# Gated cross-attention with an aux table: the value table as bf16 halves, and moves in the opening, the reloads and the last tiles

## Chip, cores and metric

The kernel runs on 1 core of a Trainium2 chip. Its time is the device time of one execution, in microseconds (us). All engine names are those of the profile: PE is TensorE, DVE is VectorE, ACT is ScalarE, POOL is GpSimd, SP issues most transfers.

## What is computed

The reference, cut to what matters:

```python
# x: (8, 224, 2048), ctx: (8, 750, 512), mask: (224, 750)
q  = layernorm(x)                                     # 32 heads of 64, ctx gives 8 key/value heads
p  = softmax(q_head @ ctx_head.T / 8 + mask)
x  = x + tanh(g_xattn) * (p @ ctx_head)               # keys and values are the same rows
h  = layernorm(x)
query = h @ Wq.T
router = (query @ Wr.T) @ (aux_keys @ Wr.T).T / sqrt(48) + log_rel     # 512 slots, the 8 highest are kept
w  = softmax(query @ aux_keys.T / 8 + log_rel over those 8)
aux = (w @ aux_values) @ Wvd.T @ Wvu.T                # 2048 -> 128 -> 2048
gate = f(var(h), gelu(h @ Wu1.T + bu1) @ Wu2.T + bu2)
x  = x + tanh(g_ffn) * (h + gate * aux)
```

## The kernel before

Each engine has its own program, written out by hand; they meet at semaphores only. What an engine does is in the order of its function, and a wait holds everything behind it.

**Attention.** The 224 rows of a batch are 128 "top" rows and 96 "rest" rows. A window is one batch and one key head (64 of them); a window has seven units of 128 query rows: four of top rows and three of rest rows. The loop variable `k` runs over the units, `place(k)` gives window and unit `m`. For a unit PE makes the scores (`score_main` L896, `score_mid` L907), DVE adds the mask and takes the maximum (L1289), ACT the exponential (L709), PE turns the result (L919, L926), ACT copies it from PSUM (L705), POOL makes the low half, that is the fp32 value less its upper 16 bits (L578), and PE multiplies both halves with the values (L943, L944, L949). Rows are normalized for a pair of windows: `norm_top` on ACT (L672), `norm_rest` on ACT (L678); for batch 0 ACT does the first 128 columns of the rest rows and POOL the other 384 (L571). The statistics of batch 0's rest rows are averaged over partitions by two small products on PE (L993, L995), with DVE steps L1206 to L1213 between and behind them. The finished rest rows go to a scratch tensor in DRAM, `spill` (L423, 12 transfers per batch).

**Aux part.** 14 tiles of 128 rows: eight of top rows, kept in SBUF, and six read back from `spill` (L485, L488). The value table `v2 = aux_values @ Wvd.T` is summed once, in `sum_v2` (L1021): eight pieces of two 128-row blocks, each piece in one of three staging slots (`load_piece`, L466 and L467), fp32 with fp32. These slots and the lower half of the tile area lie over buffers of attention. Per tile PE does `sum_wide` (L972), `sum_query` (L986), `turn_h` (L959), `route` (L1076, L1080, L1081), `turn_w` (L1060), `sum_z` (L1066); all wide operands are split into a high and a low half. DVE does the top-8 selection (`select`), ACT `gelu` (L772) and `weigh` (the softmax weights, L776), each with its own function table.

**Results.** A tile's result is `base` (ACT, L751, 128x2048) plus four parts of 512 columns: `aux_part` on PE (L1050), added by `finish` on DVE (L1391). The table `FINISH` says in which loop step `t` which tiles are finished; the parts stand at fixed places `i` = 0 to 7 of the step. All parts share PSUM bank 7, so that part `n+1` waits until DVE has added part `n`; the last two tiles, behind the loop, have banks of their own (`TAIL_BANKS`). SP stores a finished tile; quarters of the last two tiles go out from SP and ACT.

The pieces of code on which the steps below rest, where a sentence does not say it:

```python
            sum_v2(range(0, 2))      # PE, behind pe.wait_ge(x_added, GROUPS)
            sum_wide(0, 2)
            sum_query(0, 2)
            turn_h(1, 1)
            sum_v2(range(2, 4))
```

## Time and profile before

| | |
|---|---|
| median of 3 runs | 1185.97 us (1185.53 to 1186.67) |
| profiled execution, its own time | 1187.15 us |
| its span, first to last instruction | 1185.3 us |
| busy: PE, PEld | 1158.6 us (98%), 914.1 us (77%) |
| busy: DVE, ACT, POOL | 944.8 us (80%), 918.7 us (78%), 888.7 us (75%) |
| chain of waits | PE 73%, POOL 19%, DVE 3%, DMA 2% |
| DMA | 95.09 MB, mean 80 GB/s |
| from issue to landing, median | piece of the value table 5.7 us, spilled tile read back 7.4 us, spill row 2.2 us |

PEld is the loading of weights, which overlaps PE. The chain of waits follows the last instruction back to what released it, step by step; a share of it is time in which nothing else could have started the next step. Attention ends at about 888 us, the loop over tiles runs from 919 to 1171 us.

### The profile page before, as it was taken

The numbers are of one execution on the slowest core, as the hardware profiler recorded it, in microseconds if no ns is written. First come the engines' busy times: TensorE is split into PE (matmuls) and PEld (weight loads), VectorE is DVE, ScalarE is ACT, GpSimd is POOL, SyncE is SP. The second block draws the span as 40 slices with busy tenths as digits, with TensorE's granted clock in tenths as the row PEclk, the third lists the DMA queues.
The fourth block names the chain that finished last, engine by engine and source line by source line (L and its number), as shares of the span: only waits on it lengthen the run. The fifth ranks groups of instructions, "written<-read, shape, count | busy, mean of one in ns | idle before, by whom it ended". The sixth has DMA issues, their size and how long they took to land.

```text
span 1185.3 us, 35321 instructions
## 1 busy us (share of the span) xinstructions
PE 1158.6 (98%) x14642; PEld 914.1 (77%) x14642; DVE 944.8 (80%) x2255; ACT 918.7 (78%) x1230; POOL 888.7 (75%) x800
## 2 busy tenths in 40 slices
PE   5999999999999999999999999999999999999997
PEld 3888888888888888888888888888887666555553
DVE  5988888888888888888888888888864899666765
ACT  5898988888998989989899889988871444655544
POOL 5899999999999999999999999999981111403222
PEclk9999999999999999999999999999999999999999
DMA  9421231233114212321321231131227200011223
GB/s 346 124 79 48 57 116 41 55 78 100 41 42 117 73 43 61 110 55 48 98 73 43 57 71 41 42 70 53 77 95 244 108 2 1 1 72 72 107 107 142
DMA packets 60736, 95.09 MB, mean 80 GB/s; under 512 B 35234, under 2 KB 44450, under 8 KB 56483
## 3 DMA queue, kind: packets, MB, share of 16 engines
q1 hardware_dynamic: 59858, 91.79, 25.5%
q8 instruction: 118, 1.93, 0.7%
q10 hardware_dynamic: 720, 1.05, 0.3%
q14 instruction: 40, 0.32, 0.1%
HBM read 71.75 MB, written 20.97 MB: 78 GB/s over the span
## 4 chain that ended last, share of the span: by engine, by line
PE 73%; POOL 19%; DVE 3%; DMA 2%; issue 1%; ACT 1%; SPq 1%; DVEq 0%; POOLq 0%
POOL arena L578 14%; PE psum L896 12%; PE psum L919 12%; PE psum L972 11%; PE psum L926 6%; PE psum L907 6%; PE psum L949 5%; PE psum L943 5%; PE psum L944 5%; PE psum L1050 3%; POOL arena L546 2%; PE psum L986 2%; PE psum L959 2%; PE psum L874 2%; POOL arena L595 1%
## 5 line engine op out<-in xcount | busy, mean ns | idle before, releaser
L578 POOL TENSOR_TENSOR arena<-arena 128x768 bf16<-128x768 f32 x448 | 652.7, 1472 | 45.2 <-ACT arena L705 43.3
L1289 DVE CUSTOM_DVE_ANT_0 arena<-psum,arena 128x750 f32<-128x750 f32 x448 | 420.5, 939 | 129.7 <-PE psum L907 124.1
L705 ACT ACTIVATE arena<-psum 128x768 f32<-128x768 f32 x448 | 362.5, 809 | 89.4 <-PE psum L926 89.4
L709 ACT ACTIVATE arena<-arena,neg_max 128x750 f32<-128x750 f32 x448 | 410.8, 917 | 4.2 <-DVE neg_max L1289 4.2
L896 PE MATMUL psum<-arena 128*128 128x512 bf16 x896 | 272.8, 385 | 0.0
L919 PE MATMUL psum<-ident,arena 128*128 128x128 f32 x1792 | 269.2, 273 | 0.0
L943 PEld LDWEIGHTS psum<-arena 128*128 128x128 bf16 (+1 forms) x2688 | 194.7, 98 | 57.5
L944 PE MATMUL psum<-arena 128*128 128x64 bf16 (+1 forms) x2688 | 222.0, 193 | 0.0
L943 PE MATMUL psum<-arena 128*128 128x65 bf16 (+1 forms) x2688 | 221.7, 194 | 0.0
L944 PEld LDWEIGHTS psum<-arena 128*128 128x128 bf16 (+1 forms) x2688 | 178.5, 98 | 53.2
L919 PEld LDWEIGHTS psum<-ident,arena 128*128 128x128 f32 x1792 | 207.0, 141 | 5.5 <-ACT arena L709 1.1
L926 PE MATMUL psum<-ident,arena 128*128 128x128 f32 x896 | 171.5, 273 | 0.1
L907 PE MATMUL psum<-arena 128*128 128x238 bf16 x896 | 167.8, 268 | 1.8 <-DVE neg_max L1289 0.9
L972 PE MATMUL psum<-arena 128*128 128x512 bf16 x672 | 161.4, 384 | 0.0
L949 PE MATMUL psum<-arena 128*128 128x65 bf16 (+1 forms) x2688 | 160.0, 194 | 0.9 <-POOL arena L578 0.9
L972 PEld LDWEIGHTS psum<-arena 128*128 128x128 bf16 x672 | 63.6, 96 | 75.0 <-issue 0.8
L949 PEld LDWEIGHTS psum<-arena 128*128 128x128 bf16 (+1 forms) x2688 | 114.9, 98 | 1.5 <-POOL arena L578 1.4
L926 PEld LDWEIGHTS psum<-ident,arena 128*128 128x128 f32 x896 | 112.1, 141 | 0.6 <-ACT arena L705 0.4
L685 ACT ACTIVATE arena<-psum 128x512 bf16<-128x512 f32 x56 | 33.3, 597 | 99.1 <-PE psum L959 99.0
L1232 DVE SCALAR_TENSOR_TENSOR arena<-psum,r_den,arena 128x64 f32<-128x64 f32 x448 | 97.4, 277 | 2.3
L546 POOL TENSOR_TENSOR arena<-arena 128x750 bf16<-128x750 f32 x64 | 92.3, 1442 | 0.0
L896 PEld LDWEIGHTS psum<-arena 128*128 128x128 bf16 x896 | 88.1, 98 | 5.3
(160 smaller groups left out, 1270.9 us busy)
## 6 DMA issues: line engine op xcount, KB each, us to landing
arena<-in_k_t SPq DMA_DIRECT2D x128, 187.5 KB, 3.2
arena<-in_v_rows SPq DMA_DIRECT2D x64, 192.0 KB, 2.5
out<-arena SPq DMA_DIRECT2D x12, 1024.0 KB, 3.9
arena<-in_x_top SPq DMA_DIRECT2D x8, 1024.0 KB, 5.3
arena<-in_x_rest SPq DMA_DIRECT2D x8, 768.0 KB, 4.6
spill<-arena SPq DMA_DIRECT2D x96, 64.0 KB, 2.2
arena<-spill SPq DMA_DIRECT2D x6, 1024.0 KB, 7.4
arena<-in_w_t SPq DMA_DIRECT2D x4, 1024.0 KB, 19.4
```

The source lines that it names most:

```text
L578: pool.tensor_tensor(p_lo[:, n % RING, :], p_sb[:, n % RING, :], high(p_sb[:, n % RING, :]), ALU.subtract).then_inc(p_split, 1)
L705: act.activation(p_sb[:, n % RING, :], flat_ps[:, turned_at(n):turned_at(n) + CW], ACT.Copy).then_inc(evac_a, 1)
L709: act.activation(s_sb[:, n % RING, 0:CTX], s_sb[:, n % RING, 0:CTX], ACT.Exp, bias=neg_max[:, n % 4, :], scale=-1.0).then_inc(exped, 1)
L896: pe.matmul(flat_ps[:, score_at(n) + cols.start:score_at(n) + cols.stop], q_t[:, pair % 2, half, turn, :], kk, start=(i == 0), stop=(i == 1))
L907: mm = pe.matmul(flat_ps[:, score_at(n) + cols.start:score_at(n) + cols.stop], q_t[:, g // 2 % 2, half, turn, :], kk, start=(i == 0), stop ...
L919: pe.transpose(flat_ps[:, at:at + 128], s_sb[:, n % RING, c * 128:(c + 1) * 128], ident[:, :])
L926: mm = pe.transpose(flat_ps[:, at:at + 128], s_sb[:, n % RING, c * 128:(c + 1) * 128], ident[:, :])
L943: pe.matmul(o, hi, v_hi[0:rows, u, c, :], start=(c == 0), stop=False, skip_group_check=True)
L944: pe.matmul(o[:, 0:D], hi, v_lo[0:rows, u, c, :], start=False, stop=False, skip_group_check=True)
L949: mm = pe.matmul(o, lo, v_hi[0:rows, u, c, :], start=False, stop=(c == NCH - 1), skip_group_check=True)
L972: mm = pe.matmul(psum[:, 2, :], h[:, j, kk, :], w, start=(k == 0 and n == 0), stop=(k == KC - 1 and n == 2))
L1289: dve.tensor_tensor_reduce(s_sb[:, n % RING, 0:CTX], flat_ps[:, score_at(n):score_at(n) + CTX], mask_sb[:, max(n % UNITS - REP + 1, 0), :] ...
```

## The change

1. The value table is summed from halves. GpSimd makes the low halves of each piece (`split_piece`: three subtractions), after the last batch's rows have been spilled; PE runs three bf16 products where one fp32 product was. PE no longer waits for the load of a piece but for `v2_split`. The pieces stand at other places: 2, 3, 2, 1 instead of 2, 2, 2, 2.
2. SP reads the first three spilled tiles back after the last piece's load, not between the pieces.
3. Opening: ACT's `norm_rest` of batch 0 and its `norm_top(1)` go to POOL, under the new semaphores `rest_first` and `top_second`; the second averaging product comes after the first unit's scores.
4. In step t=1 ACT does `weigh(0)` ahead of `gelu(0)`.
5. Result part 5 is added before the split and the next rows of the step, not after them.
6. Tile 11 is finished behind the loop, with tiles 12 and 13; twelve parts there use seven banks in turn; DVE's and ACT's last steps are in another order.

```diff
-FINISH = {8: (0, 1), 9: (2, 3), 10: (4, 5), 11: (6, 7), 12: (8, 9), 13: (10, 11), 14: (12, 13)}
+FINISH = {8: (0, 1), 9: (2, 3), 10: (4, 5), 11: (6, 7), 12: (8, 9), 13: (10,), 14: (11, 12, 13)}
...
+        TAIL = FINISH[TILES]
+        TAIL_SEQ = (7, 0, 1, 3, 4, 5, 2, 7, 0, 1, 3, 4)
+        TAIL_BANKS = {(u, n): TAIL_SEQ[4 * i + n] for i, u in enumerate(TAIL) for n in range(4)}
...
@@ SP
             for i in range(STAGE_SLOTS, KC // 2):
                 sp.wait_ge(v2_piece, i - STAGE_SLOTS + 1)
                 load_piece(i)
-                if i - STAGE_SLOTS in (0, 2, 4):
-                    u = (i - STAGE_SLOTS) // 2
-                    sp.dma_start(x2b[:, u, :], spill[128 * u:128 * u + 128]).then_inc(x2_loaded[u], 16)
-            sp.wait_ge(v2_piece, KC // 2)
-            for i in range(3, B_TILES):
+            for i in range(B_TILES):
+                if i == 3:
+                    sp.wait_ge(v2_piece, KC // 2)
                 sp.dma_start(x2b[:, i, :], spill[128 * i:128 * i + 128]).then_inc(x2_loaded[i], 16)
...
@@ POOL
-            for j in range(NB):
-                pool.tensor_scalar(xn_rest[:, j, 2 * D:], xb[:, 0, j, 2 * D:], ln_scale[:, 1 + j:2 + j], ln_bias[:, 1 + j:2 + j],
-                                   ALU.mult, ALU.add).then_inc(rest_widened, 1)
+            for cols, done in ((slice(0, 2 * D), rest_first), (slice(2 * D, KV * D), rest_widened)):
+                for j in range(NB):
+                    pool.tensor_scalar(xn_rest[:, j, cols], xb[:, 0, j, cols], ln_scale[:, 1 + j:2 + j], ln_bias[:, 1 + j:2 + j],
+                                       ALU.mult, ALU.add).then_inc(done, 1)
...
+                if m == 2 and window == -1:
+                    pool.tensor_scalar(xn_top[:, 1, :], xa[:, 0, 2 * GW:4 * GW], ln_scale[:, 0:1], ln_bias[:, 0:1],
+                                       ALU.mult, ALU.add).then_inc(top_second, 1)
...
+            def split_piece(i):
+
+                slot = i % STAGE_SLOTS
+                pool.wait_ge(v2_loaded[slot], 32 * (1 + i // STAGE_SLOTS))
+                if i >= STAGE_SLOTS:
+                    pool.wait_ge(v2_piece, i - STAGE_SLOTS + 1)
+                for kk in range(2):
+                    pool.tensor_tensor(av_lo[:, slot, kk, :], av_stage[:, slot, kk, :], high(av_stage[:, slot, kk, :]),
+                                       ALU.subtract).then_inc(v2_split, 1)
+                pool.tensor_tensor(wvd_lo[:, slot], wvd_stage[:, slot], high(wvd_stage[:, slot]), ALU.subtract).then_inc(v2_split, 1)
+
+            pool.wait_ge(spilled[(BATCH - 1) % 3], 16 * REP * NB * ((BATCH - 1) // 3 + 1))
+            for i in range(KC // 2):
+                split_piece(i)
...
@@ ACT
-                if k == -4:
-                    for j in range(NB):
-                        norm_rest(0, j)
...
-                if m == 6 and window == -1:
-                    norm_top(1)
...
-                gelu(t - 1)
                 if t == 1:
                     weigh(0)
+                gelu(t - 1)
...
-            store_quarter(TILES - 2, 1)
             act.wait_ge(last_clipped, 1)
             act.activation(last_col[:, 4:5], last_col[:, 3:4], ACT.Exp, bias=scal_neg[:, 2:3], scale=scal_neg[:, 1:2]).then_inc(last_exped, 1)
+            store_quarter(TILES - 2, 1)
...
@@ PE
-            pe.wait_ge(own_step, 3)
-            pe.matmul(psum[:, 3, 0:NB], quad[:, :], own_sum[:, :], start=True, stop=True).then_inc(own_spread, 1)
...
+                if k + 5 == 0:
+                    pe.wait_ge(own_step, 3)
+                    pe.matmul(psum[:, 3, 0:NB], quad[:, :], own_sum[:, :], start=True, stop=True).then_inc(own_spread, 1)
...
-                    pe.wait_ge(v2_loaded[i % STAGE_SLOTS], 32 * (1 + i // STAGE_SLOTS))
+                    slot = i % STAGE_SLOTS
+                    pe.wait_ge(v2_split, 3 * i + 3)
                     for kk in range(2):
+                        wide = high(wvd_stage[:, slot, kk, :])
                         for m in range(4):
-                            mm = pe.matmul(psum[:, 6, m * 128:(m + 1) * 128], av_stage[:, i % STAGE_SLOTS, kk, m * 128:(m + 1) * 128],
-                                           wvd_stage[:, i % STAGE_SLOTS, kk, :], start=(i == 0 and kk == 0 and m == 0),
+                            cols = slice(m * 128, (m + 1) * 128)
+                            values = high(av_stage[:, slot, kk, cols])
+                            pe.matmul(psum[:, 6, cols], values, wide, start=(i == 0 and kk == 0 and m == 0), stop=False, skip_group_check=True)
+                            pe.matmul(psum[:, 6, cols], values, wvd_lo[:, slot, kk, :], start=False, stop=False, skip_group_check=True)
+                            mm = pe.matmul(psum[:, 6, cols], av_lo[:, slot, kk, cols], wide, start=False,
                                            stop=(i == KC // 2 - 1 and kk == 1), skip_group_check=True)
                     mm.then_inc(v2_piece, 1)
...
-            sum_v2(range(2, 4))
+            sum_v2(range(2, 5))
             sum_wide(0, 3)
             sum_query(0, 3)
             turn_h(1, 2)
-            sum_v2(range(4, 6))
+            sum_v2(range(5, 7))
             turn_h(1, 3)
             route(0)
-            sum_v2(range(6, 8))
+            sum_v2(range(7, 8))
...
-            for i in range(4):
-                if i == 0:
+            for i in range(4 * len(TAIL)):
+                if i == 1:
                     turn_w(TILES - 1)
                 aux_part(TILES, i)
-                if i == 1:
+                if i == 3:
                     sum_z(TILES - 1)
...
@@ DVE
                 split_z(t - 1)
+                finish(t, 5)
                 late_stats(t, 6)
                 if t + 1 < TILES:
                     split_h(t + 1, 2)
                 if t + 2 < TILES:
                     stage_h(t + 2, 0)
-                finish(t, 5)
...
             finish(TILES, 0)
+            finish(TILES, 1)
             dot(TILES - 1)
-            finish(TILES, 1)
-            split_z(TILES - 1)
+            finish(TILES, 2)
+            finish(TILES, 3)
             dve.wait_ge(last_exped, 1)
...
-            finish(TILES, 2)
+            split_z(TILES - 1)
+            finish(TILES, 4)
             dve.wait_ge(last_exped, 2)
...
-            for i in range(3, 8):
+            for i in range(5, 4 * len(TAIL)):
                 finish(TILES, i)
```

PE's order where attention has ended, before: `wr_rows` is the router's product, L1021 are the value table's products, L972 the wide products of tile 0.

```order
L959 MATMUL psum<-ident,arena 128x128 x3
L1092 MATMUL psum<-arena,wr_rows 64x512 [waits rk_ready]
L1021 MATMUL psum<-arena 128x128 [waits v2_loaded0,x_added]
L1021 MATMUL psum<-arena 128x128 x7
L1021 MATMUL psum<-arena 128x128 [waits v2_loaded1]
L1021 MATMUL psum<-arena 128x128 x7
L972 MATMUL psum<-arena 128x512 [waits w1_split,h_split]
```

And of the change; the three lines L1060 to L1062 (high by high, high by low, low by high) come eight times per piece, two pieces in a row, before the same wide products.

```order
L993 MATMUL psum<-ident,arena 128x128 x3
L1134 MATMUL psum<-arena,wr_rows 64x512 [waits rk_ready]
L1060 MATMUL psum<-arena 128x128 [waits v2_split,x_added]
L1061 MATMUL psum<-arena 128x128
L1062 MATMUL psum<-arena 128x128
```

The products stand where they stood, with three instructions for one, and their wait is now for GpSimd. On POOL, behind the low half of the keys, the change has these (before, the statistics of tile 3, `ga<-mv_all`, follow at once):

```order
L629 TENSOR_TENSOR keys_lo<-arena,keys_hi 128x512 [waits keys_split]
L638 TENSOR_TENSOR arena<-arena 128x512 [waits v2_loaded0,spilled1]
L638 TENSOR_TENSOR arena<-arena 128x512
L640 TENSOR_TENSOR arena<-arena 128x256
L638 TENSOR_TENSOR arena<-arena 128x512 [waits v2_loaded1]
L638 TENSOR_TENSOR arena<-arena 128x512
L640 TENSOR_TENSOR arena<-arena 128x256
```

The first of them waits for the last spilled rows (`spilled1`). The third place is DVE in a step with results, before:

```order
L1395 TENSOR_TENSOR arena<-psum,arena 128x128 [waits z_ready]
L1279 TENSOR_TENSOR arena<-psum,arena 128x512 [waits h_hi_done]
L1260 TENSOR_SCALAR arena<-arena,mv_all,rstd_all 128x512 [waits h_turned,rstd2_done]
L1391 SCALAR_TENSOR_TENSOR arena<-psum,aux_scale,arena 128x512 [waits aux_summed] x2
L1370 TENSOR_TENSOR arena<-psum,arena 128x512 [waits dotted,w1_quarter]
```

and of the change, where one of the two additions stands ahead of the split (L1319) and the next rows (L1300):

```order
L1435 TENSOR_TENSOR arena<-psum,arena 128x128 [waits z_ready]
L1431 SCALAR_TENSOR_TENSOR arena<-psum,aux_scale,arena 128x512 [waits aux_summed]
L1319 TENSOR_TENSOR arena<-psum,arena 128x512 [waits h_hi_done]
L1300 TENSOR_SCALAR arena<-arena,mv_all,rstd_all 128x512 [waits h_turned,rstd2_done]
L1431 SCALAR_TENSOR_TENSOR arena<-psum,aux_scale,arena 128x512 [waits aux_summed]
L1410 TENSOR_TENSOR arena<-psum,arena 128x512 [waits dotted,w1_quarter]
```

## Rows read from the trace of the kernel before

**Rows 1.** Chain of waits, opening; columns: start us, us, what.

```profile
14.43 0.59 PE psum L995 x2
15.01 0.88 PE psum L896 x2
15.89 0.41 PE psum L907 x2
...
16.47 0.94 DVE arena L1289
...
23.50 0.73 PE psum L919 x4
...
29.21 0.44 PE psum L919 x4
```

**Rows 2.** Windows, opening; columns: stretch, us, busy per engine, PEclk, DMA share, GB/s.

```profile
22.00:24.00 2.00, 2.00 (x10) 1.62 (x9) 1.13 (x3) 1.92 (x4) 1.25 (x1) 1.00 1.03 430
```

**Rows 3.** Timeline, opening; start us, us, engine line op [idle before <-releaser].

```profile
17.11 1.97 POOL L571 TENSOR_SCALAR arena<-arena,ln_scale,ln_bias 128x384 f32<-128x384 f32 x3
18.28 1.25 ACT L678 ACTIVATE arena<-arena,ln_bias,ln_scale 128x128 f32<-128x128 f32 x3
22.75 1.47 POOL L578 TENSOR_TENSOR arena<-arena 128x768 bf16<-128x768 f32 x1 [2.82 <-ACT arena L705]
27.56 0.20 PEld L926 LDWEIGHTS psum<-ident,arena 128*128 128x128 f32 x2 [0.36 <-ACT arena L705]
```

**Rows 4.** Timeline, change of stage.

```profile
893.82 3.84 PE L1021 MATMUL psum<-arena 128*128 128x128 f32 x32
899.50 0.33 SPq L466 DMA_DIRECT2D arena<-in_av_t  x1
903.21 2.05 PE L1021 MATMUL psum<-arena 128*128 128x128 f32 x16 [0.21 <-DMA arena<-in_wvd_t]
915.47 3.84 PE L1021 MATMUL psum<-arena 128*128 128x128 f32 x32 [0.40 <-DMA arena<-in_wvd_t]
921.91 0.69 DVE L1343 CUSTOM_DVE_ANT_0 arena<-arena 128x512 f32<-128x512 f32 x1 [2.14 <-ACT arena L772]
924.06 0.66 PE L1060 MATMUL psum<-ident,arena 128*128 128x128 f32 x4 [0.31 <-ACT arena L776]
```

**Rows 5.** Windows, step t=10: us, PE, PEld, DVE, ACT, POOL busy, PEclk.

```profile
1083.43:1106.29 22.86, 22.33 (x140) 12.52 (x137) 15.55 (x29) 11.83 (x16) 6.15 (x18) 1.00 0.23 93
```

**Rows 6.** Timeline, change of stage, VectorE beside GpSimd.

```profile
889.39 1.60 POOL L606 TENSOR_SCALAR arena<-arena 128x512 f32<-128x512 f32 x1 [4.71 <-PE psum L1087]
891.04 1.47 DVE L1260 TENSOR_SCALAR arena<-arena,mv_all,rstd_all 128x512 f32<-128x512 f32 x1
```

**Rows 7.** Chain of waits, change of stage and t=10.

```profile
905.66 9.76 DMA arena<-in_wvd_t
...
1094.53 0.86 PE psum L1076 x2
...
1105.62 0.67 PE psum L1050 x3
1106.29 1.34 PE psum L986 x24
```

**Rows 8.** Groups of GpSimd, whole span: line, names, shapes, count, busy us, mean ns, idle.

```profile
L578 POOL TENSOR_TENSOR arena<-arena 128x768 bf16<-128x768 f32 x448 | 652.7, 1472 | 45.2 <-ACT arena L705 43.3
...
L595 POOL TENSOR_TENSOR arena<-arena 128x512 bf16<-128x512 f32 x16 | 16.8, 1050 | 0.2
```

**Rows 9.** Timeline, step t=10.

```profile
1101.76 0.54 DVE L1260 TENSOR_SCALAR arena<-arena,mv_all,rstd_all 128x512 f32<-128x512 f32 x1
...
1103.01 0.84 PE L1050 MATMUL psum<-arena 128*128 128x512 bf16 x3 [0.53 <-DVE arena L1391]
```

**Rows 10.** Timeline, tail.

```profile
1172.04 0.63 ACT L772 ACTIVATE arena<-arena 128x512 f32<-128x512 f32 x1 [1.72 <-DVE arena L1370]
...
1178.11 3.38 DVE L1391 SCALAR_TENSOR_TENSOR arena<-psum,aux_scale,arena 128x512 f32<-128x512 f32 x5
```

More of the change, by code:

```diff
@@ L187, in flamingo_block @@
         wvd_stage = slots[:, :, 2 * NSLOT:2 * NSLOT + 2 * VB].rearrange("p s (k n) -> p s k n", k=2)
+        lo_at = stage_at + STAGE_SLOTS * (2 * NSLOT + 2 * VB)
+        lo_slots = arena[:, lo_at:lo_at + STAGE_SLOTS * (NSLOT + VB)].bitcast(BF16).rearrange("p (s n) -> p s n", s=STAGE_SLOTS)
+        av_lo = lo_slots[:, :, 0:2 * NSLOT].rearrange("p s (k n) -> p s k n", k=2)
+        wvd_lo = lo_slots[:, :, 2 * NSLOT:2 * NSLOT + 2 * VB].rearrange("p s (k n) -> p s k n", k=2)
+        assert lo_at + STAGE_SLOTS * (NSLOT + VB) <= used["ffn"]
         v2 = carve("ffn", [128, 4, VB])
@@ L250, in flamingo_block @@
         rest_normed = sem("rest_normed")
+        rest_first = sem("rest_first")
+        top_second = sem("top_second")
         spilled = [sem(f"spilled{i}") for i in range(3)]
@@ L285, in flamingo_block @@
         v2_ready = sem("v2_ready")
+        v2_split = sem("v2_split")
         preact_done = sem("preact_done")
@@ L382, in parts_before, with tail_user @@
             return 4 * ORDER.index(u) + n
-        TAIL_BANKS = {(TILES - 2, 0): 7, (TILES - 2, 1): 0, (TILES - 2, 2): 1, (TILES - 2, 3): 3,
-                      (TILES - 1, 0): 4, (TILES - 1, 1): 5, (TILES - 1, 2): 2, (TILES - 1, 3): 7}
+        TAIL = FINISH[TILES]
+        TAIL_SEQ = (7, 0, 1, 3, 4, 5, 2, 7, 0, 1, 3, 4)
+        TAIL_BANKS = {(u, n): TAIL_SEQ[4 * i + n] for i, u in enumerate(TAIL) for n in range(4)}
+        def tail_user(u, n):
+            at = 4 * TAIL.index(u) + n
+            users = [k for k in range(at) if TAIL_SEQ[k] == TAIL_SEQ[at]]
+            return users[-1] if users else None
         def aux_ps(u, n):
@@ L532, in factors @@
                 pool.wait_ge(ln_ve_done, i + 1)
+                if i == 2:
+                    pool.wait_ge(top_second, 1)
+                    pool.wait_ge(rest_widened, NB)
                 if i >= 2:
-                    pool.wait_ge(top_normed, 4 * (i - 1))
-                    pool.wait_ge(rest_normed, NB * (i - 1))
+                    pool.wait_ge(top_normed, 4 * (i - 1) - 1)
+                if i >= 3:
+                    pool.wait_ge(rest_normed, NB * (i - 2))
                 pool.tensor_tensor(ln_scale[:, cols], ln_ve[:, cols], ln_half[:, cols], ALU.pow).then_inc(ln_scale_done, 1)
@@ L823, in _ @@
                 round_z(t - 1)
-                if len(bases) > 1:
-                    base(bases[1])
+                for u in bases[1:]:
+                    base(u)
                 if t + 1 < TILES:
@@ L848, in turn_first @@
                 if i == 1:
-                    pe.wait_ge(rest_normed, NB)
+                    pe.wait_ge(rest_first, NB)
                 if i == 2:
@@ L855, in turn_q @@
                 pair = window // 2 + 1
-                pe.wait_ge(top_normed, pair + 1)
-                pe.wait_ge(rest_normed, NB * (pair // 4) + (2 if pair % 4 == 0 and window % 2 == 0 else NB))
+                if pair == 1:
+                    pe.wait_ge(top_second, 1)
+                else:
+                    pe.wait_ge(top_normed, pair)
+                if pair >= 4:
+                    pe.wait_ge(rest_normed, NB * (pair // 4 - 1) + (2 if pair % 4 == 0 and window % 2 == 0 else NB))
                 if window == 0:
@@ L1036, in aux_part @@
                 bank = TAIL_BANKS.get((u, n), 7)
-                if bank == 7 and parts_before(u, n) >= 1:
-                    last = parts_before(TILES - 2, 1) if (u, n) == (TILES - 1, 3) else parts_before(u, n)
-                    pe.wait_ge(y_added, last)
+                again = tail_user(u, n) if u in TAIL else None
+                if again is not None:
+                    pe.wait_ge(y_added, parts_before(TAIL[0], again + 1))
+                elif bank == 7 and parts_before(u, n) >= 1:
+                    pe.wait_ge(y_added, parts_before(u, n))
                 elif bank in (0, 1):
@@ L1141, in _ @@
                 aux_part(t, 7)
-            for i in range(4):
-                if i == 0:
+            for i in range(4 * len(TAIL)):
+                if i == 1:
                     turn_w(TILES - 1)
                 aux_part(TILES, i)
-                if i == 1:
+                if i == 3:
                     sum_z(TILES - 1)
-            for i in range(4, 8):
-                aux_part(TILES, i)
         @block.vector
```

3 lines of the change are left out of this document (1 added, 2 removed).

## The prediction

> **What bounds the kernel now.** I read the page first: TensorE is busy for 98% of the span, and in the chain of waits it holds 73%, GpSimd 19%. TensorE's busy sum cannot tell how full it is, so I went stage by stage, with the chain, then the timeline, then the windows. Four places matter, and the reader should see in each what the next instruction waited for.
>
> *Opening.* The chain goes through the two small averaging products. TensorE issues L995, then the first score products L896 and L907, and at 23.50 four transposes (L919) still take 0.73 us; the same four take 0.44 us at 29.21 [rows 1]. So TensorE works at its lower level, 1.2 GHz, until about 24 us, although the column of the granted clock says 1.00 there [rows 2]. GpSimd and ScalarE share the normalizing [rows 3].
>
> *Attention* is bound by TensorE, with GpSimd on the chain in the middle. No instruction there changes, so a shift of the opening carries through.
>
> *The change of stage* (893.8 to 924 us). TensorE runs the value table: 128 float products in eight pieces, 32 of them in 3.84 us. It hardly waits: 0.21 and 0.40 us for pieces to land, 0.31 us for the softmax weights. The spilled rows have landed at 899.50, where SP goes on [rows 4].
>
> *The tiles with results* (t=8 to 12) take 22.86 us where TensorE is busy for 22.33 us [rows 5].
>
> **1. Opening: -1.2 us.** L995 leaves its place ahead of the first scores. It waited for VectorE (L1210) until 14.43, and L896 came on the chain at 15.01. The first score product needs the first L1186 only, three steps before L1210, so scores can start more than 1 us earlier. But VectorE still waits for L995 before it takes the first maximum; L995 now runs behind 0.88 + 0.41 us of scores, from about 14.7 to 15.1; VectorE copies (0.16 us) and starts at 15.35 instead of 16.47 [rows 1]: 1.1 us. The later steps follow in the same rhythm. ScalarE loses 1.25 us of norms, so no exponential is late, and GpSimd takes them: three of 128 columns (L571's 0.66 us for 384 give about 0.35 each), then, after the wide ones, a row of 512 columns, 0.9 to 1.6 us by L571 and L606 [rows 3, 6]. It comes to its first low half at about 22.3 us, where before it was 22.75, after 2.82 us of waiting: covered by that wait. The norm of the second pair, also taken from ScalarE, ends an idle 0.36 us of TensorE at 27.56 [rows 3]. Against this, if the clock rises at 24 us as before, the time won at half rate counts half. Between 0.5 and 1.6 us I take 1.2.
>
> **2. The value table: +6.5 us.** TensorE's own work falls: 192 products of two-byte halves at 1.34/24 = 0.056 us are 10.7 us, for 128 of 3.84/32 = 0.120, 15.4 us [rows 4, 7]. But the first piece stood ready at 893.82 and now waits for GpSimd, and GpSimd waits for the spilled rows, 899.50. A piece is two subtractions of 512 columns and one of 256: 1.05 us each, and 1.05 less 256 columns at (1.47-1.05)/256, 0.63 us [rows 8]; back to back a little less, as each starts while the last one ends. I take 2.6 us a piece. With 3.7 us from a freed slot to a landed piece (SP at 899.50, TensorE at 903.21, [rows 4]) I follow both engines:
> - GpSimd has pieces 0, 1, 2 at 902.2, 904.8, 907.4. TensorE, which has had nothing since 893.82, starts at 902.2. At half rate piece 0 ends at 904.9 and piece 1 at 907.5.
> - Their slots are loaded again by 908.6 and 911.2, so GpSimd has pieces 3 and 4 at 911.2 and 913.8. TensorE does the wide products (2.67), the query (0.44) and a transpose (0.44), a part of it still slowly, until 911.5, then pieces 2, 3, 4 until 915.5.
> - Slots again: GpSimd has pieces 5, 6, 7 at 919.1, 921.7, 924.3. TensorE: next block until 919.1, piece 5 until 920.4, piece 6 until 923.1, transpose and routing (0.44 + 0.86 + 0.43, [rows 7]) until 924.8, piece 7 until 926.2.
>
> Before, the last piece ended at 919.3. That is 6.9 us; SP no longer puts a megabyte of spilled rows between two pieces (that made one land after 9.76 us, [rows 7]), so I say 6.5. Ends: with every load hidden GpSimd alone gives 899.5 + 7 x 2.5, then 1.34 + 1.75 + 1.34, 921.5: +2.2. With landings of 5 us and a half rate as long as in the opening, near 930: +10. The spilled rows themselves are needed tens of microseconds later and cost nothing.
>
> GpSimd and VectorE also hinder each other: L1260 took 1.47 us beside a GpSimd step and 0.54 alone, and L606 took 1.60 [rows 6, 9]. Some three L1260 fall into the pieces, at 0.5 us each. The Trainium skill ("SBUF — State Buffer", "SBUF: two separate sides") says the same port pair is held for a whole instruction and the loser blocks; by that rule the sum would be 0.5 to 1.5 us more than by free engines.
>
> What TensorE does after an empty stretch no row here shows but the start, where it was slow until 24 us though it had worked since 14.43 [rows 1]; therefore half rate at first. The Trainium skill ("TensorE: Matmul & The Clock Gate", "The HAM clock gate") says that an idle array falls to half its clock and must be kept busy to get it back; it speaks against a change that empties TensorE for 8 us.
>
> **3. Weights ahead of gelu in tile 1: +1.7 us.** ScalarE now does the weights of tile 0 first, and a table load goes. But the selection (3.7 us on VectorE) now starts only when the table is done, as routing stands behind piece 6. So, counted from the end of the table: selection until +3.7, weights +4.6, table load 1.28 and gelu 0.63 until +6.5. VectorE's dot product starts there; before it started 2.6 us behind the table (921.91) [rows 4]. From dot to joined query VectorE has 3.6 us of work (three statistics or dots of 0.69, a split of 0.69, the next rows 0.54, the join 0.28), so q_ready comes at +10.1. TensorE is at route(1) at +8.7 (before, it found it ready). That is 1.4 us, and 0.3 us more as VectorE, nearly full in these tiles, catches up. Ends 0 and 2.5.
>
> **4. Result part 5 ahead of the split: -2.9 us.** Part 6 shares a bank with part 5 and waits until VectorE has added it: VectorE comes to it behind L1279 and L1260 (from 1101.76), and TensorE starts at 1103.01 after 0.53 us idle [rows 9]. Put first, it is done 1.2 us sooner and the wait goes. The wait is 0.53 us, and the restarted product shows 0.84 us where the next takes 0.67 in the chain [rows 7, 9]: 0.7, four times, and 0.1 to 0.3 in t=12. What becomes later (split and next rows) is needed a quarter of a tile on. Ends -2.0 and -3.1.
>
> **5. The tail: -0.5 us.** Tile 11 moves behind the loop: TensorE leaves it 2.67 us earlier. Gelu does not follow, since ScalarE now has a third base (2.08 us) ahead of the weights and two table loads of 1.28 behind: done at about 1171.2, before 1172.7 [rows 10]. VectorE then holds the end: 12 parts at 3.38/5 = 0.68, preactivation, dot, and eight small steps of 0.2 [rows 10]. I get the last part done at 1180.8 instead of 1181.5, and seven quarter rows in a row for the queues instead of five. Ends -1.5 and +0.8.
>
> **Sum:** -1.2 + 6.5 + 1.7 - 2.9 - 0.5 = +3.6. The profiled execution took 1187.15 us, 1.2 above the median of the runs; I put the difference on the median 1185.97: 1189.6 us. A measurement of this kernel can tell about 0.2%, 2.4 us, from no change.
>
> **Rivals.**
> *A, the clock stays high* over the empty stretch. Then piece 0 ends at 903.5, its slot is full at 907.2, GpSimd never waits for a load until piece 5, and piece 7 ends at 924.1: +4.8; with the third term at 1.2 the sum is +1.4, 1187.4 us, no change. For: the column shows 1.00 throughout. Against: it shows 1.00 in the slow opening too. Chance 0.2. The rule of the Trainium skill cited above ("TensorE: Matmul & The Clock Gate") speaks against it as well.
> *B, GpSimd keeps ahead of TensorE* and the gains come in full. If loads are hidden the table ends at 921.5 (+2.2), and if the early weights just absorb the wait the third term is 0; with -1.6, -3.1 and -1.2 elsewhere: -3.7, 1182.3 us, faster. It decides as soon as the table ends less than about 3 us later than before. For: slots turn over faster without the spilled rows between. Against: slot 0 is free only after piece 0, and GpSimd starts at 899.5 at best. Chance 0.14.
> *C, the stage costs more*: landings near the median 5.7 of these loads or blocked GpSimd, +10 for the table instead of +6.5: 1193.1 us. Chance 0.17.
> *D, the moved part gains nothing*, because the wait only passes on to the split behind it: the sum without -2.9 is +6.5, 1192.5 us. The slack of VectorE (15.55 of 22.86 busy, [rows 5]) speaks against it. Chance 0.08.
>
> **Numbers.** My forecast has 0.41, with 1187.5 to 1191.5 of its own. C and D are slower; A is no change, and so is the low edge of the forecast, some 0.08; B faster. Faster 0.14, same 0.28, slower 0.58. From 1184 (which leaves out most of B) to 1194 about 8 in 10 lie.
>
> **What would show it.** In the changed profile: first maximum near 15.4 us; TensorE empty for 8 us before its first table piece, which then takes about 2.7 us where the last takes 1.34; table end 6 to 7 us later, set against the end of attention; a wait of 1 to 2 us at the second routing; tiles t=8 to 11 at 22.2 us; the end of VectorE 12 us behind the last wide product. I am wrong if TensorE waits less than 5 us for GpSimd, or if the table ends less than 4 us later.

## The result, and the profile after

| | before | changed |
|---|---|---|
| median of 16 runs | 1185.76 us (1183.77 to 1186.83) | 1188.50 us (1187.75 to 1188.96) |
| ratio | | 1.0024, 95% interval 1.0016 to 1.0032 |
| span of the profiled run | 1185.3 us | 1186.4 us |
| GpSimd busy | 888.7 us | 911.1 us |

The change is slower by 2.7 us; 1189.6 was forecast, 1.1 more. One execution of run 2 took 4212 us and is left out of its ratio. Lines of the changed kernel: score products L930 and L941, transposes L953 and L960, attention's last value products L983, averaging product L1045, maximum L1329, low halves of a piece L638 and L640, table products L1060 to L1062, copy of the finished table L834, wide products L1006, query products L1020, piece loads L481 and L482, gelu L802, weights L806, routing L1118, the joined query's addition L1414, dot L1383, preactivation L1410, result parts L1092, their sums L1431.

Timeline of the kernel before, the two marks between which the value table lies:

```profile
886.52 0.36 PE L949 MATMUL psum<-arena 128*128 128x65 bf16 x6
...
919.34 0.60 ACT L804 ACTIVATE arena<-psum 128x512 f32<-128x512 f32 x1 [4.93 <-PE psum L1021]
```

Timeline of the changed kernel: opening, change of stage, steps t=1 and t=2, step t=10, tail (start us, us, engine line op, idle before and what ended it):

```profile
13.68 1.01 PE L930 MATMUL psum<-arena 128*128 128x512 bf16 x2 [0.79 <-DVE arena L1226]
...
14.88 0.44 PE L1045 MATMUL psum<-own_sum,quad 128*128 128x3 f32 x2
...
15.52 0.94 DVE L1329 CUSTOM_DVE_ANT_0 arena<-psum,arena 128x750 f32<-128x750 f32 x1
...
19.23 0.60 PE L953 MATMUL psum<-ident,arena 128*128 128x128 f32 x4
...
23.63 0.44 PE L960 MATMUL psum<-ident,arena 128*128 128x128 f32 x2 [0.69 <-ACT arena L740]
...
884.12 0.36 PE L983 MATMUL psum<-arena 128*128 128x65 bf16 x6
...
895.89 2.04 POOL L638 TENSOR_TENSOR arena<-arena 128x512 bf16<-128x512 f32 x2 [6.07 <-DMA spill<-arena]
...
898.65 0.26 PE L1060 MATMUL psum<-arena 128*128 128x128 bf16 x1 [7.17 <-POOL arena L640]
...
901.44 0.33 SPq L481 DMA_DIRECT2D arena<-in_av_t  x1
...
906.50 2.04 POOL L638 TENSOR_TENSOR arena<-arena 128x512 bf16<-128x512 f32 x2 [2.86 <-DMA arena<-in_wvd_t]
...
907.75 1.07 DVE L1300 TENSOR_SCALAR arena<-arena,mv_all,rstd_all 128x512 f32<-128x512 f32 x1
...
908.50 0.80 POOL L640 TENSOR_TENSOR arena<-arena 128x256 bf16<-128x256 f32 x1
...
909.35 0.23 PE L1060 MATMUL psum<-arena 128*128 128x128 bf16 x1 [1.51 <-POOL arena L640]
...
911.92 0.23 PE L1060 MATMUL psum<-arena 128*128 128x128 bf16 x1 [1.03 <-POOL arena L640]
...
922.97 0.60 ACT L834 ACTIVATE arena<-psum 128x512 f32<-128x512 f32 x1 [2.16 <-PE psum L1062]
...
928.99 0.69 DVE L1383 CUSTOM_DVE_ANT_0 arena<-arena 128x512 f32<-128x512 f32 x1 [2.82 <-ACT arena L802]
...
932.17 1.13 PE L1118 MATMUL psum<-arena 128*128 128x512 f32 x2 [0.81 <-DVE arena L1414]
...
943.00 2.60 PE L1006 MATMUL psum<-arena 128*128 128x512 bf16 x11 [0.75 <-DVE arena L1410]
...
1105.84 0.83 PE L1092 MATMUL psum<-arena 128*128 128x512 bf16 x3
...
1172.19 0.63 ACT L802 ACTIVATE arena<-arena 128x512 f32<-128x512 f32 x1
...
1177.87 4.70 DVE L1431 SCALAR_TENSOR_TENSOR arena<-psum,aux_scale,arena 128x512 f32<-128x512 f32 x7
```

The windows of the changed kernel, TensorE's hole, its end, and step t=10 (us, then busy time of PE, PEld, DVE, ACT, POOL, then the granted clock, DMA share, GB/s):

```profile
894.00:897.00 3.00, 0.00 (x0) 0.00 (x0) 0.94 (x3) 0.00 (x0) 1.10 (x2) 0.64 0.27 47
897.00:900.00 3.00, 1.35 (x14) 1.38 (x15) 0.00 (x0) 0.00 (x0) 3.00 (x4) 0.50 0.00 0
...
1086.96:1109.11 22.15, 21.97 (x137) 12.57 (x138) 15.55 (x29) 11.83 (x16) 6.13 (x18) 1.00 0.23 95
```

Read in order of time: the first maximum starts at 15.52, where it was 16.47 [rows 1]. From the end of L1134 near 891.5 TensorE has nothing for 7.17 us, because GpSimd starts only when the spilled rows have landed; the granted clock falls to 0.50, the 1.2 GHz level. The finished table is copied out at 922.97, where it was at 919.34. In step t=10 the wait ahead of the result part (0.53 us, [rows 9]) is gone and the step takes 22.15 us instead of 22.86 [rows 5].

So each stage can be booked, set against the same marks in both profiles:

| stage, mark at its end | before | changed | difference | forecast |
|---|---|---|---|---|
| attention's last value products start | 886.52 | 884.12 | -2.40 | -1.2 |
| from there to the copy of the table | 32.82 | 38.85 | +6.03 | +6.5 |
| from there to step t=3 | 33.98 | 35.28 | +1.30 | +1.7 |
| steps t=8 to 12 | 113.82 | 110.75 | -3.07 | -2.9 |
| from there to VectorE's last sum | 30.11 | 29.33 | -0.78 | -0.5 |

The rest is equal, and the sum is +1.1, the difference of the spans. The medians stand 2.7 apart, 1.6 more. Some 1.0 of that lies in the first line, as the first run below shows; the rest of it is booked to no stage.

### The profile page after: what moved, and what is told of

Its sections match the earlier page's. It is cut to its first block, busy times and chain, and to the rows that moved or that the text cites. A ratio compares the mean times of both kernels' runs of the same rounds, so it can differ in the third digit from the quotient of the medians.

```text
span 1186.4 us, 35222 instructions
## 1 busy us (share of the span) xinstructions
PE 1136.7 (96%) x14449; PEld 910.4 (77%) x14706; DVE 945.3 (80%) x2255; ACT 916.4 (77%) x1226; POOL 911.1 (77%) x828
## 4 chain that ended last, share of the span: by engine, by line
PE 71%; POOL 20%; DVE 3%; issue 2%; DMA 2%; ACT 1%; SPq 1%; DVEq 0%; POOLq 0%
POOL arena L596 14%; PE psum L953 12%; PE psum L1006 11%; PE psum L930 11%; PE psum L960 6%; PE psum L941 6%; PE psum L983 5%; PE psum L977 5%; PE psum L978 5%; PE psum L1092 3%; POOL arena L563 2%; PE psum L993 2%; PE psum L908 2%; PE psum L1020 2%; POOL arena L616 1%
## 5 line engine op out<-in xcount | busy, mean ns | idle before, releaser
L1329 DVE CUSTOM_DVE_ANT_0 arena<-psum,arena 128x750 f32<-128x750 f32 x448 | 420.5, 939 | 126.8 <-PE psum L941 121.3
L953 PE MATMUL psum<-ident,arena 128*128 128x128 f32 x1792 | 268.4, 272 | 0.0
L930 PE MATMUL psum<-arena 128*128 128x512 bf16 x674 | 221.9, 384 | 14.9 <-DVE arena L1226 0.8
L953 PEld LDWEIGHTS psum<-ident,arena 128*128 128x128 f32 x1792 | 206.4, 140 | 4.3
L960 PE MATMUL psum<-ident,arena 128*128 128x128 f32 x896 | 171.3, 273 | 0.7 <-ACT arena L740 0.7
L941 PE MATMUL psum<-arena 128*128 128x238 bf16 x896 | 167.3, 267 | 1.0 <-DVE neg_max L1329 1.0
L983 PE MATMUL psum<-arena 128*128 128x65 bf16 (+1 forms) x2688 | 160.1, 194 | 1.4 <-POOL arena L596 1.4
L1006 PE MATMUL psum<-arena 128*128 128x512 bf16 x648 | 156.8, 384 | 2.2 <-DVE arena L1410 0.7
L1006 PEld LDWEIGHTS psum<-arena 128*128 128x128 bf16 x672 | 63.5, 96 | 75.6 <-issue 1.5
L983 PEld LDWEIGHTS psum<-arena 128*128 128x128 bf16 (+1 forms) x2688 | 114.9, 98 | 2.1 <-POOL arena L596 2.0
L960 PEld LDWEIGHTS psum<-ident,arena 128*128 128x128 f32 x896 | 112.0, 141 | 1.2 <-ACT arena L740 1.1
L930 PEld LDWEIGHTS psum<-arena 128*128 128x128 bf16 x896 | 87.7, 98 | 6.1 <-issue 0.8
```

Source lines behind the costliest of these rows:

```text
L930: pe.matmul(flat_ps[:, score_at(n) + cols.start:score_at(n) + cols.stop], q_t[:, pair % 2, half, turn, :], kk, start=(i == 0), stop=(i == 1))
L941: mm = pe.matmul(flat_ps[:, score_at(n) + cols.start:score_at(n) + cols.stop], q_t[:, g // 2 % 2, half, turn, :], kk, start=(i == 0), stop ...
L953: pe.transpose(flat_ps[:, at:at + 128], s_sb[:, n % RING, c * 128:(c + 1) * 128], ident[:, :])
L960: mm = pe.transpose(flat_ps[:, at:at + 128], s_sb[:, n % RING, c * 128:(c + 1) * 128], ident[:, :])
L983: mm = pe.matmul(o, lo, v_hi[0:rows, u, c, :], start=False, stop=(c == NCH - 1), skip_group_check=True)
L1006: mm = pe.matmul(psum[:, 2, :], h[:, j, kk, :], w, start=(k == 0 and n == 0), stop=(k == KC - 1 and n == 2))
```

## The experiments

All ratios are against the kernel before, with 95% intervals. "The table's time" is from the start of attention's last value products to the start of the copy of the table: 32.82 us before, 38.85 in the change.

**1. The opening alone** (averaging product behind the scores, norms on GpSimd).

> Before with the opening of the change alone. Theory 1 (the forecast's term; the profiled run of before was a run whose TensorE went over to full rate late, at about 24 us, and most runs are not like it): -1.2 us against the median of before, ratio 0.9990, between 0.9986 and 0.9996. Theory 2 (the ledger of the two profiles holds for all runs): -2.4 us, ratio 0.9980. In its profile the first maximum starts near 15.5 us and the last value product of attention ends near 884.1 us.

Measured 0.9992 (0.9983 to 1.0001), -0.9 us by the ratio and -0.6 between the two medians (1185.03 and 1185.62). First maximum at 15.59, attention's end at 884.87. The kernels of this study and the two of the case give eleven profiles with the new opening and three with the old: attention ends at 884.12 to 884.87 in ten of the new (885.95 in one), mean 884.54, and at 885.30, 886.14 and 886.52 in the old, mean 885.99. That is -1.4 us, and the profiled run of before was the latest of its kind. Theory 1 is nearer; the -2.4 of the table above does not hold for all runs.

**2. Result part 5 alone.**

```
     split_z(t - 1)
+    finish(t, 5)
     late_stats(t, 6)
...
-    finish(t, 5)
```

> Before with result part 5 ahead of the split, nothing else. Theory (the forecast's fourth term): steps t=8 to 11 take 22.15 us instead of 22.86, together -2.8 to -3.1 us, ratio 0.9975. Rival (the wait passes on to the split or to the next rows): steps stay within 0.2 us of 22.86, ratio 1.000.

Measured 0.9976 (0.9966 to 0.9986), -2.8 us by the ratio, as expected. Windows of this kernel, step t=10, the stretch that answers to [rows 5]:

```profile
1081.46:1103.60 22.14, 22.14 (x139) 12.58 (x137) 15.55 (x29) 11.82 (x16) 6.14 (x18) 1.00 0.23 96
```

VectorE's work is the same 15.55 us; only its order went, and TensorE has no idle time left in the step.

**3. The value table alone**, everything else as before.

> Before with the value table in halves (its pieces on GpSimd, three products, pieces grouped 2, 3, 2, 1, spilled rows read back behind the pieces) and the order gelu, then weights, kept. Theory: the table ends 6.0 us later set against the end of attention, as in the whole change; +6.0 to +7.5 us, ratio 1.0055. Rival (much of the stage's loss in the whole change comes from its combination with the weights ahead of gelu): +4 us or less, ratio 1.003.

Measured 1.0053 (1.0041 to 1.0066), +6.7 us by the medians; the table's time is 39.33 us, 6.5 more than before. The loss is all in the table. Over all profiles of these two designs the float table takes 32.73 to 33.48 us (four profiles: before and runs 1, 2 and 4) and the table of the change 38.85 to 39.33 us (three: the change and runs 3 and 5), so the term is +6.0 us in the mean.

**4. Everything but the table and the gelu order.**

> The change with the value table and the order of weights and gelu put back as before; opening, result part 5 and tail as changed. If the ledger's terms add up (opening -1.0 to -2.4, part 5 -3.1, tail -0.8): -4.9 to -6.3 us, ratio 0.9953. If the gains need the other half of the change (for instance VectorE has to be late for them): -2 us or less, ratio 0.998.

Measured 0.9959 (0.9946 to 0.9971), -4.8 us. The terms add up: steps t=8 to 12 at 22.15 us, the tail 29.32 us from its mark, 29.33 in the whole change. The other parts are gains on their own, and the table eats them.

**5. Gelu ahead of the weights again.**

```
+    gelu(t - 1)
     if t == 1:
         weigh(0)
-    gelu(t - 1)
```

> The change with gelu of tile 0 ahead of its weights again in step t=1, nothing else. Theory 1 (the weights ahead of gelu delay VectorE's dot, the joined query and so the second routing; this is the +1.3 us of the ledger between the end of the table and t=3): -1.0 to -1.7 us against the whole change, that is ratio 1.0012 against before, and no idle time of TensorE at the second routing. Theory 2 (the loss comes from the selection, which starts only when the table is done whichever comes first): no difference, ratio 1.0024, and the wait at the second routing stays.

Measured 1.0009 (1.0000 to 1.0018), where the whole change has 1.0024. Timeline of this kernel, steps t=1 and t=2:

```profile
926.47 0.69 DVE L1383 CUSTOM_DVE_ANT_0 arena<-arena 128x512 f32<-128x512 f32 x1
...
927.96 0.66 PE L1102 MATMUL psum<-ident,arena 128*128 128x128 f32 x4 [0.31 <-ACT arena L806]
...
932.01 1.02 PE L1118 MATMUL psum<-arena 128*128 128x512 f32 x2
...
941.74 2.83 PE L1006 MATMUL psum<-arena 128*128 128x512 bf16 x12
```

The dot comes 2.5 us earlier though the table ends 0.3 later; both waits of the change (0.81 and 0.75 us) are gone, and one of 0.31 us for the weights is back. t=1 and t=2 take 17.35 and 16.82 us, where the change takes 17.90 and 17.58, together 1.31 more. The intervals of the two ratios overlap; it is the stages of the profiles that tell the two kernels apart. The selection is as late here, so theory 2 falls.

**6. GpSimd waits for attention's sums, not for the spilled rows.**

```
-    pool.wait_ge(spilled[(BATCH - 1) % 3], ...)
+    pool.wait_ge(x_added, GROUPS)
     for i in range(KC // 2):
         split_piece(i)
```

> The change, but GpSimd waits before its first piece for the end of attention's sums (VectorE's last addition) instead of the spilled rows. Theory 1 (the wait for the spilled rows is what empties TensorE, and the low halves don't lie over the spilled rows): GpSimd starts at about 889.9 us instead of 895.9, TensorE waits about 1 us instead of 7.2, the table ends 6 to 7 us earlier than in the change: ratio 0.9970 against before. Theory 2 (GpSimd's 2.6 us a piece and the 4 to 5 us of a load bound the table in any case): 2 to 3 us, ratio 1.0000.

Measured 0.9974 (0.9964 to 0.9984), -5.5 us against the change's 1188.5. Timeline of this kernel:

```profile
890.06 2.22 POOL L638 TENSOR_TENSOR arena<-arena 128x512 bf16<-128x512 f32 x2
...
893.19 0.22 PE L1060 MATMUL psum<-arena 128*128 128x128 bf16 x1 [1.43 <-POOL arena L640]
...
917.87 0.60 ACT L834 ACTIVATE arena<-psum 128x512 f32<-128x512 f32 x1 [2.28 <-PE psum L1062]
```

GpSimd starts at 890.06, TensorE's first wait is 1.43 us, and the table's time is 33.47 us instead of 38.85. Theory 1 holds. Counted from the start of the shared part of the kernel's buffer `arena`, in words of 4 bytes, the low halves take 13056 to 14976, which attention uses for keys and values, and the rows to be spilled lie at 16904 to 21512. So this wait guarded nothing, and 5.7 of the 7.17 us of the hole came from it. What follows the table did not change: t=1 and t=2 still take 17.78 and 17.58 us.

**7. SP does not wait for them either** before it loads pieces; it waits before it reads the spilled rows back.

```
-    sp.wait_ge(spilled[(BATCH - 1) % 3], ...)
     for i in range(STAGE_SLOTS, KC // 2):
         ...
+    sp.wait_ge(spilled[(BATCH - 1) % 3], ...)
     for i in range(B_TILES):
```

> As the kernel before this one, and SP does not wait for the spilled rows either before it loads the fourth piece. Theory 1: the loads of the fourth and fifth piece are issued 2 us earlier and the table ends about 1.5 us earlier still, ratio 0.9957. Theory 2 (those loads share the queues with the spill and land no earlier, or hold up the spill): no difference from the kernel before this one.

Measured 0.9962 (0.9950 to 0.9975); the table's time is 31.76 us, 1.7 less. This is what theory 1 says.

**8. A filler in the hole.**

```
     pe.wait_ge(x_added, GROUPS)
+    for _ in range(28):
+        pe.matmul(psum[:, 7, :], wq_cat[:, 0, :], wq_cat[:, 0:4, :], start=True, stop=True)
     sum_v2(range(0, 2))
```

> The change with 28 more products of 512 columns of constants, into a bank that nobody reads there, between the wait for attention's sums and the first table piece, so that TensorE is busy while GpSimd makes its first piece. Theory 1 (the half rate of the first table piece, 0.107 us a product instead of 0.056, comes from TensorE having been idle for 7.2 us): the first piece takes 1.34 us instead of 2.7, and its slot is free 1.3 us sooner: -1.0 to -1.4 us against the change, ratio 1.0013 against before. Theory 2 (the half rate comes from something else, GpSimd and VectorE reading at the same time, for instance): the first piece takes 2.7 us as before, ratio 1.0024.

Measured 1.0024 (1.0015 to 1.0033), as theory 2 has it; but its profile contradicts theory 2. Timeline and windows of this kernel, first and seventh piece:

```profile
900.38 0.23 PE L1060 MATMUL psum<-arena 128*128 128x128 bf16 x1 [0.93 <-POOL arena L640]
...
920.27 0.23 PE L1060 MATMUL psum<-arena 128*128 128x128 bf16 x1 [2.64 <-POOL arena L640]
```

```profile
897.00:900.00 3.00, 2.46 (x12) 0.90 (x10) 0.00 (x0) 0.00 (x0) 2.28 (x3) 1.00 0.06 9
900.00:903.00 3.00, 1.58 (x25) 1.41 (x26) 0.00 (x0) 0.00 (x0) 3.00 (x5) 1.00 0.06 11
...
921.00:923.00 2.00, 2.00 (x19) 2.00 (x18) 0.00 (x0) 0.00 (x0) 1.93 (x4) 0.50 0.99 397
```

The clock stays at 1.00, the first piece's products come every 0.056 us and its slot is freed 1.3 us sooner, so theory 1 is right on the clock. The gain is lost further on: the load of the seventh piece, issued at 910.81, landed only at 917.37, TensorE stood still for 2.64 us, and then the clock fell here. The table's time is 40.62 us in this profile, against 38.85 in the change. The 11 executions spread: the three with a mean granted clock of 0.997 took 1190.1 to 1191.7 us, the four with 0.998, the profiled one among them, 1188.2 to 1191.3, the four with 0.999 or 1.000 took 1187.0 to 1188.3. The last group is 0.2 to 1.5 us below the change's median. That the slowest pay for such a second fall fits the one profile, but is not shown for the others.

**9. The filler, with all reads of the spilled rows behind the table.**

```
+    sp.wait_ge(v2_piece, KC // 2)
     for i in range(B_TILES):
-        if i == 3:
-            sp.wait_ge(v2_piece, KC // 2)
```

> The kernel with the 28 filler products, and all six reads of the spilled rows put behind the last table piece (three of them stood ahead of it). Theory 1 (in the filler's run the three megabytes of spilled rows, issued right behind the last piece's load, held that load and the one before it back; GpSimd had the seventh piece late, TensorE stood empty for 2.64 us and lost the gain of the first piece there): the loads of the seventh and eighth piece land within 5 us, no wait of TensorE over 1.5 us remains behind the fourth piece, and the table ends 37.0 to 37.8 us after the end of attention instead of 40.6 (and 38.85 in the change): ratio 1.0012. Theory 2 (three piece loads close together delay each other, the spilled rows have no part): the table ends 40 us or more after attention, ratio 1.0024 again.

Measured 1.0024 (1.0015 to 1.0034). The seventh piece's load landed 6.7 us after its issue again and TensorE waited 2.84 us, with nothing of the spill in the queues; the table's time was 39.11 us. The guess about the spilled rows falls. Theory 2 is nearer, but why this load is so slow stays open: it follows another by 1.36 us in both runs, and so it does in runs 7 and 10, where it had landed within 5.0 us. There the next load follows 3.2 and 2.4 us later, here and in run 8 it follows 1.9 us later; this fits theory 2, and no run changes that distance alone. After the 2.84 us the granted clock stayed at 1.00 in this profile, and again the executions part: 0.999 with 1186.6 to 1188.9 us, 0.997 with 1189.9 to 1190.8. Windows of this kernel, the stretch where the one before had 0.50:

```profile
921.00:923.00 2.00, 1.95 (x21) 1.28 (x21) 1.45 (x3) 0.51 (x1) 1.13 (x3) 1.00 0.00 0
```

**10. Both early starts, gelu first, reads of the spilled rows last.**

> The kernel whose GpSimd and SP don't wait for the spilled rows (ratio 0.9962), with gelu ahead of the weights again and the reads of the spilled rows behind the last piece. The gelu order was worth 1.7 us, so ratio 0.9948; if the spilled rows held the last loads back here too, up to 1.5 us more, 0.9937. Rival: with an earlier table the order of gelu and weights no longer matters, and the ratio stays at 0.996.

Measured 0.9953 (0.9941 to 0.9966). The table's time is 32.23 us; t=1 and t=2 take 17.36 and 16.81 us, in run 7 17.90 and 17.58: the order of gelu matters here as well. Whether the later reads bring anything cannot be read from this profile, because the clock fell in it. Timeline of this kernel, then the windows of this kernel and of run 7:

```profile
892.99 0.22 PE L1059 MATMUL psum<-arena 128*128 128x128 bf16 x1 [1.43 <-POOL arena L639]
```

```profile
894.00:896.00 2.00, 1.68 (x17) 1.41 (x16) 1.01 (x3) 0.00 (x0) 2.00 (x3) 0.50 0.43 76
```

```profile
894.00:896.00 2.00, 1.04 (x19) 0.87 (x17) 1.18 (x3) 0.00 (x0) 2.00 (x4) 1.00 0.59 103
```

TensorE waits 1.43 us for the first piece in runs 6, 7 and 10; only in the last did the granted clock fall behind it. The slot of the second piece is free 0.7 us later there than in run 7, counted from the end of attention, and the table ends 0.5 us later.

**11. The first two pieces as float products**, so GpSimd begins with the third.

```
+    if i < 2:
+        pe.wait_ge(v2_loaded[slot], 32)
+        ...
+        continue
```

> As the kernel before this one, with the first two pieces of the table as float products (as before the change), so that TensorE has them without GpSimd and GpSimd begins with the third. Worked out from the runs: TensorE begins the table 7.35 us after the end of attention without a wait, two pieces take 3.84 us, and no wait over 1 us is left; the table ends near 29.5 us after the end of attention, where the whole float table ends at 33.4 and the kernel without waits for the spilled rows at 31.8. Ratio 0.9925 (near 1177 us). Rival (the loads bound the stage: 3.7 to 5 us from a free slot, three slots): it ends no earlier than 31.5, ratio 0.994 or above.

Measured 0.9962 (0.9949 to 0.9975), five executions from 1179.3 to 1183.4 us. Timeline of the fastest:

```profile
891.51 3.84 PE L1057 MATMUL psum<-arena 128*128 128x128 f32 x32
...
899.00 2.04 POOL L637 TENSOR_TENSOR arena<-arena 128x512 bf16<-128x512 f32 x2 [6.13 <-DMA arena<-in_wvd_t]
...
901.85 0.23 PE L1068 MATMUL psum<-arena 128*128 128x128 bf16 x1 [1.58 <-POOL arena L639]
...
904.42 0.23 PE L1068 MATMUL psum<-arena 128*128 128x128 bf16 x1 [1.03 <-POOL arena L639]
```

The table's time is 31.15 us, between the two expectations; the ratio is where the rival has it, and no better than in run 10. The load issued at 894.40 took 4.6 us (I had counted 3.7), and its two waits of TensorE were not in my working. The fastest execution had a mean clock of 1.000, the others 0.998 and 0.997.

**12. The fourth and fifth piece float too.**

> As the kernel with two float pieces, with the fourth and fifth piece float too, so that GpSimd makes only the third, sixth, seventh and eighth. Both places where TensorE stood still there (1.58 and 1.03 us, for the fourth and fifth piece) waited for GpSimd, which waited for a load. Theory 1: these pieces now wait for their landing alone; TensorE's work grows by 2 x 0.58 us, the two waits go (2.6 us), the table ends near 30.1 us after the end of attention instead of 31.15, and as TensorE nowhere stands still for over 0.5 us, all executions have it at full rate in this stage and lie within 1.5 us of each other (the kernel with two float pieces spread over 4.1 us, its fastest execution alone with a mean granted clock of 1.000): ratio 0.9933, near 1178 us. Theory 2 (the spread has another cause, or the loads are the bound in any case): ratio 0.995 to 0.996 and a spread of 3 us or more.

Measured 0.9943 (0.9929 to 0.9956), 1179.57 us, the lowest median of the study: 6.6 us below the kernel before on the same chip and some 9 below the change. Its interval overlaps those of runs 10 and 11. The table's time is 30.85 us with one wait of TensorE (1.21 us), where 30.1 and none were expected; the executions lie within 1.1 us of each other. The spread is that of theory 1, but it does not show that stops of TensorE make a spread: run 10 has stops too and spreads over 1.3 us. The level was 1.5 us too low in my expectation.

## Why the prediction was right, and where it was off

**1. Opening, -1.2.** By the medians of its own run -0.6, by the ends of attention -1.4: right. The first maximum came at 15.52 for 15.35, since TensorE's first transposes themselves started 0.2 us later (12.01 for 11.81). The step "if the clock rises at 24 us as before" did not hold: the four transposes first take 0.60 us at 19.23 here. In the fourteen profiles that moment lies at 18.9 to 19.2 us in three, at 21.1 to 21.3 in two and at 22.5 to 24.9 in nine. What the early rise brought was partly spent in a wait for ScalarE at 23.63, and over the profiles with the new opening the end of attention does not follow it: 884.83 us with the rise at 19.22 (run 12), 884.21 with 23.96 (run 11). What sets that end stays open.

**2. The table, +6.5.** Measured +6.03 in the change and +6.5 alone. The mechanism was as worked out: GpSimd at 2.57 us a piece for 2.6, TensorE empty for 7.17 us for 8.4, the first piece at half rate in 2.7 us for 2.7. Two terms of the sum were off and cancelled, which is luck. The spilled rows had landed 9.4 us after the first of them was issued (886.49 to 895.89), not 10.6 (888.89 to 899.50 before), so GpSimd began 1.2 us earlier; why is not known. And a freed slot was full again after 3.7 us in some cases (910.92 to at most 914.58), after 5.1 in others (901.44 to 906.50), and after 6.6 in run 8. Runs 6 and 7 show what my working took as given: it followed GpSimd's wait for the spilled rows without asking whether these rows lie where the low halves go. That wait was the cause of 5.4 us of the loss (38.85 to 33.47), which was 6.0 us. The 0.4 us that I took off because no megabyte of spilled rows goes between two pieces was tested by no run alone.

The half rate was argued from the start of the kernel alone, and rival A set against it. Rows now show it: 0.50 granted after the hole, 1.00 with the filler. The rule of the Trainium skill ("TensorE: Matmul & The Clock Gate", "The HAM clock gate"), that an idle array falls to half its clock, agrees with these rows. Run 10 shows half the clock behind a stop of 1.43 us too. Rival A's price for a clock that stays (table 2.1 us less) was not reached: the filler's better executions gained 1.5 us at most. A longer stay at half rate cost little in the one pair of profiles that shows it: in run 5's the clock reads 0.50 until 904 us, in the change until 901.6, and the table takes 39.03 us for 38.85.

What VectorE and GpSimd cost each other was smaller than the 0.5 to 1.5 us that the prediction put beside the rule of the Trainium skill ("SBUF — State Buffer", "SBUF: two separate sides"): over all pieces one L640 took 0.80 us instead of 0.61, beside an L1300 of 1.07, and one pair of L638 2.21 instead of 2.04. VectorE has little to do there (it is idle for 12.17 and 8.85 us), since it waits for the TensorE that waits for GpSimd.

**3. Weights ahead of gelu, +1.7.** The term was mis-sized by little: +1.30 in the profile, and run 5 puts it at 1.2 to 1.8 us. The wait at the second routing was 0.81 us and not 1.4. I had added 0.3 us for the time in which VectorE catches up; in its place there is a second wait of 0.75 us, in t=2, for the preactivation. That run 5 takes back the whole term shows that the order costs it; my sentence that the late selection starts it all names the occasion and not the cause.

**4. Part 5, -2.9.** -3.07 in the change, -2.8 alone. Four steps of 0.70 and 0.25 in t=12, as worked out. Rival D falls.

**5. Tail, -0.5.** -0.78: VectorE's last sum ends 29.33 us after the last mark instead of 30.11. Gelu ends 19.58 us after that mark (1172.82), before 21.29: -1.7 for the -1.5 of the working.

The sum of the terms was +3.6, the medians stand at +2.7 (interval 1.9 to 3.8). Every term has the forecast sign and, with -1.4 for the opening, lies within 0.5 us of it. Rival B needed GpSimd to keep ahead of TensorE, and C a stage of +10; run 6, at -3.1 us by its ratio for B's -3.7, shows that B was one wait away from being true.

## What to carry to other kernels

Before a wait is priced, look up which memory it guards: here one line, needed by no data, made a stage of halves 6 us slower than one of floats, and without it both took the same (33.47 us in run 6, 32.73 to 33.48 with floats). An order of two steps on one engine is worth a run of its own: gelu first was worth 1.3 us here, whether the table came late (run 5) or early (run 10).

An idea that is not proven: an operand that a slower engine must first prepare should not be the first that TensorE needs, even if what is ready costs more (a piece in floats 1.92 us, in halves 1.34). With two float pieces first the table was 1.1 us shorter in the profile (31.15 us in run 11, 32.23 in run 10), but run 10's first pieces ran partly at half rate, and the ratios of runs 10 to 12 (0.9953, 0.9962, 0.9943) have overlapping intervals.

## What the runs showed of the hardware that was not expected

- What follows a stop of TensorE is not settled by its length. After 2.64 us the clock went to the 1.2 GHz level (run 8, 0.50 in 921 to 923), after 2.84 us it did not (run 9, 1.00). After 1.43 us it did in run 10 (0.50 in 894 to 896) and did not in runs 6 and 7; after 1.51 and 1.03 us in the change and 2.00 us in run 6 it stayed at 1.00.
- The executions of runs 8 and 9 spread over 4.8 and 4.2 us with nothing changed. Those with a mean granted clock of 0.997 are some 3 us slower than those with 0.999; what is cause there is not shown.
- The four transposes of the opening first take 0.60 us (1.06 at half rate) anywhere from 18.9 to 24.9 us; the column of the granted clock says 1.00 from 14 to 24 us in all fourteen profiles. One profile of each kernel misjudged the opening by 1 us (-2.4 for -1.4).
- A piece of 640 KB in two transfers landed after 3.7 to 6.7 us; the slowest took 6.6 us with three megabytes of spilled rows issued behind it (run 8) and 6.7 us without them (run 9). What decides was not found.
